# Dividing attention outputs by their row sums: the reciprocal moved from ScalarE to GpSimd

## The chip, the cores and the metric

The kernel runs on one core of a Trainium2 chip. The metric is the device time of one execution in microseconds (us). Shown are the median of three runs, their spread, and the span of one profiled execution.

## The reference, cut to what matters

A chain of six residual blocks works on x, 2 sequences of 1024 tokens with 128 features: mixture of experts, attention, the same mixture of experts again, a latent-attention block with its own routed experts, a scan block, and the latent-attention block again. The blocks that matter here are the three attentions with 16 heads and causal masks:

```python
attn = softmax(where(causal, q @ k.T * scale + bias, -inf), axis=-1)
out = attn @ v                 # per head
x = x + out.reshape(b, s, d) @ W_O
...
att = softmax(where(tril, q @ k.T / sqrt(64), -inf), axis=-1)
y = (att @ v).reshape(b, t, H * D) @ Wo
```

Each softmax ends in a division by the row's sum. The kernel does that division last, on the outputs of `attn @ v`.

## The kernel before, in words

The program is written engine by engine, and each engine has a fixed order of instructions with semaphores between engines. For the attention stages the order comes from a planner, the classes `Plan` (line 95 on), `First` (the first attention) and `Late` (the experts after it, the two latent attentions, their experts and the scan). `Plan.quad` (line 131) lists the tasks of four heads ("a quad", number n) of one batch, in two phases ph of 512 queries. `Plan.simulate` (line 224) then plays the engines forward with the costs in `COST` (lines 108 and 328), in us, and the priorities in `ORDER` (lines 113 and 342), and keeps the order that comes out. `Late.TABLE` (line 340) says which activation table a ScalarE task needs; `Late.extra` (line 588) charges 1.3 for a change.

There are 24 quads, 8 in `First` and 16 in `Late`, so 48 phases. In each phase:

- TensorE makes unmasked scores to find each query's maximum (`un`, line 1277), VectorE reduces them (`red`, lines 1396 to 1403), TensorE turns the maxima (`turn`, line 1343), VectorE copies them (`ct`, line 1418) and two small DMAs on SP's queue put them beside the queries (`crow`, line 1442).
- TensorE makes the scores with the maximum taken off (`sc`, line 1291, with masks in line 1298), in pairs of PSUM banks of which there are three, shared with `un`. ScalarE takes the exponential of each pair into PR (`exp`, line 1369), 18 per quad and 432 in all. TensorE multiplies PR with the values (`pv`, line 1337); a column of ones in the values gives the row sum in the same PSUM tile.
- ScalarE copies the result to OS (`ev`, line 1377); VectorE's shuffle spreads each head's row sum over its 32 partitions into RX (`den`, line 1422); ScalarE takes RX's logarithm (`ln`, line 1381) and the exponential of minus that (`rx`, line 1385); GpSimd multiplies OS with RX (`on`, line 1437), into ON for even quads and in place for odd ones.
- After each odd quad TensorE projects both quads with two matmuls (`proj`, lines 1348 and 1349), and VectorE adds the result to the residual (`add`, line 1430).

An `ev` of an odd quad waits for the `on` of the even one before it, in the same phase, since both use OS. An even quad's `on` waits for the projection before it. On GpSimd, `on` shares the queue with `vs` (copies of the values, line 1527) in `First`, and in `Late` with the gating of experts (`et`, line 2262), rotations of the queries (`rot`, lines 2282 to 2285), low parts of fp16 splits (`xql`, `xl`) and the scan's products. All elementwise tiles here are 128 partitions by 512 or 1024 elements.

```python
            last = ("pv", n, ph, NGRP[ph] - 1)
            self.take(("pv", n, ph, 0), "misc", add("ACT", "ev", ("ev", n, ph), last, ("on" if n % 2 else "proj", n - 1, ph) if n else None))
            add("DVE", "den", ("den", n, ph), ("ev", n, ph))
            add("ACT", "ln", ("ln", n, ph), ("den", n, ph))
            add("ACT", "rx", ("rx", n, ph), ("ln", n, ph))
            add("POOL", "on", ("on", n, ph), ("rx", n, ph), ("proj", n - 1, ph) if n and n % 2 == 0 else None)
```

Of the kernel before, what the change touches and what calls it, by code (L numbers as in the profile page):

```python
# [23 lines left out]
ALU = mybir.AluOpType  # L24
ACT = mybir.ActivationFunctionType
AX = mybir.AxisListType

P = 128
# [71 lines left out]
class Plan:  # L100
# [4 lines left out]
    LATENT = False  # L105
    ROOM = {"pair": 3, "misc": 2, "nr": 2}
    SINGLE = ("turn", "proj")
    COST = {"turn": 0.2, "proj": 1.9, "m4": 0.25, "ct": 0.27, "crow": 1.2, "den": 0.72, "ev": 0.58, "ln": 0.63,
            "rx": 0.63, "on": 1.27, "add": 0.68, "qk": 1.75, "qkh": 1.02, "qkl": 1.22, "val": 1.9, "vc": 1.02, "vs": 0.5,
            "put": 7.0}  # L110
    LAND = {"crow": 2.5, "put": 4.0}
    MODE = {"sc": 1, "un": 1, "pv": 2}
    ORDER = {"ACT": ("qkh", "ev", "vc", "ln", "exp", "rx"),
             "DVE": ("ct", "m4", "den", "qkl", "add", "red"),
             "POOL": ("vs", "on"),
             "SP": ("crow", "put")}
# [6 lines left out]
    def add(self, eng, stream, task, *needs):  # L123
        self.needs[task] = [x for x in needs if x is not None]
        self.streams.setdefault((eng, stream), []).append(task)
        return task
# [4 lines left out]
    def quad(self, n, units, values, first_add=(None, None)):  # L131

        add = self.add
        for ph in range(2):
            for i in range(len(UNITS[ph])):
                u = add("PE", "un", ("un", n, ph, i), *units)
                r = add("DVE", "red", ("red", n, ph, i), u)
                self.take(u, "pair", r)
            add("DVE", "m4", ("m4", n, ph), r, ("turn", n - 1, ph) if n else None)
            tn = add("PE", "turn", ("turn", n, ph), ("m4", n, ph))  # L140
            self.take(tn, "misc", add("DVE", "ct", ("ct", n, ph), tn, ("crow", n - 1, ph) if n else None))
            add("SP", "crow", ("crow", n, ph), ("ct", n, ph))
            for i in range(len(SCORES[ph])):
                g = group_of_step(ph, i)
                old = self.group_before(group(n, ph, g) - NPR)
                s = add("PE", "sc", ("sc", n, ph, i), ("crow", n, ph))
                x = add("ACT", "exp", ("exp", n, ph, i), s, ("pv",) + old if old else self.values_room(group(n, ph, g)))
                self.take(s, "pair", x)
                if i % 2 == 0 and i + 1 < len(SCORES[ph]):
                    continue  # L150
                need = [x]
                if g == 0:
                    need += values
                add("PE", "pv", ("pv", n, ph, g), *need)
            last = ("pv", n, ph, NGRP[ph] - 1)
            self.take(("pv", n, ph, 0), "misc", add("ACT", "ev", ("ev", n, ph), last, ("on" if n % 2 else "proj", n - 1, ph) if n else None))
            add("DVE", "den", ("den", n, ph), ("ev", n, ph))
            add("ACT", "ln", ("ln", n, ph), ("den", n, ph))
            add("ACT", "rx", ("rx", n, ph), ("ln", n, ph))
            add("POOL", "on", ("on", n, ph), ("rx", n, ph), ("proj", n - 1, ph) if n and n % 2 == 0 else None)  # L160
            if n % 2 == 0:
                continue
            s = add("PE", "proj", ("proj", n, ph), ("on", n, ph))
            self.take(s, "misc", add("DVE", "add", ("add", n, ph), s, first_add[ph]))
# [156 lines left out]
class Late(Plan):  # L321
# [17 lines left out]
    LAND = dict(Plan.LAND, egb=2.4, wl1=4.0, wl2=3.0, kput=3.0, st=2.5)  # L339
    TABLE = {"eg": "gelu", "si": "silu", "sg": "sigmoid", "th": "sigmoid", "ge": "gelu", "exp": "exp", "ln": "exp", "rx": "exp",  # L340
             "vln": "exp", "vex": "exp", "ve0": "exp", "rex": "exp", "de": "exp", "dl": "exp", "dx": "exp"}
    ORDER = {"ACT": ("exh", "ewh", "eg", "roth", "krh", "lath", "kh", "vc", "ev", "rex", "sq", "vln", "vex", "si", "xp", "sg", "th", "ab", "de",
                     "dl", "dx", "ge", "xh", "ln", "exp", "rx", "xqh", "wqh", "ve0", "gwh"),
             "DVE": ("exl", "ewl", "eup", "eh", "ct", "m4", "den", "cen", "scl", "scb", "rt", "gtc", "hf", "gt", "mya", "mup", "cv", "dt0", "dts", "bd",
                     "scn", "st2", "st3", "oup", "fya", "fup", "krot", "krl", "kl", "ksw", "km", "rotd", "rotl", "swp",
                     "bt", "latl", "cp", "add", "red", "gwl", "wql"),
# [287 lines left out]
def build_program(nc, a, out):  # L634
    with ExitStack() as ctx:
# [219 lines left out]
        def pool_const(pool):  # L855
# [33 lines left out]
            for e in range(E):  # L889
                ins = pool.memset(desc[:, e:e + 1], float(E - e))  # L890
            pool.memset(epsc[:, 0:1], EPS)
            ins = pool.memset(epsc[:, 1:2], EPS * EPS)
            ins.then_inc(s_const, 1)

# [296 lines left out]
        def hq(ph):  # L1191
            return slice(ph * TT, (ph + 1) * TT)
# [109 lines left out]
        def pe_attn(pe, lat, c, plan, task):  # L1302
# [37 lines left out]
            elif kind == "turn":  # L1340
                n, ph = args
                pe.wait_ge(sig["m4"], c("m4", n, ph))
                pe.transpose(single(plan, task)[0:16, 0:P], M4[:, ph, :], identf[:, :]).then_inc(sig["turn"], 1)
            else:
                n, ph = args
                pe.wait_ge(sig["on"], c("on", n, ph))
                w_o = wo1 if lat else wo0
                pe.matmul(single(plan, task), w_o[:, n % NQ - 1, :], ON[:, hq(ph)], start=True, stop=False)
                pe.matmul(single(plan, task), w_o[:, n % NQ, :], OS[:, hq(ph)], start=False, stop=True).then_inc(sig["proj"], 1)

        def act_attn(act, lat, c, plan, task):
            kind, args = task[0], task[1:]
            if kind == "exp":
# [13 lines left out]
                    dst = PR[:, slot % NPR, :, 0:256].rearrange("a (p w) t -> a w p t", w=2)  # L1367
                    src = ps[pair][:, :, :].rearrange("a w (p t) -> a w p t", p=2)
                act.activation(dst, src, ACT.Exp, scale=0.125 if lat else 1.0).then_inc(sig["exp"], 1)  # L1369
            elif kind == "ev":  # L1370
                n, ph = args
                act.wait_ge(sig["pv"], c("pv", n, ph, NGRP[ph] - 1))
                if n % 2:
                    act.wait_ge(sig["on"], c("on", n - 1, ph))
                elif n:
                    act.wait_ge(sig["proj"], c("proj", n - 1, ph))
                act.copy(OS[:, hq(ph)], single(plan, ("pv", n, ph, 0))).then_inc(sig["ev"], 1)
            elif kind == "ln":
                n, ph = args
                act.wait_ge(sig["den"], c("den", n, ph))  # L1380
                act.activation(RX[:, hq(ph)], RX[:, hq(ph)], ACT.Ln).then_inc(sig["ln"], 1)
            else:
                n, ph = args
                act.wait_ge(sig["ln"], c("ln", n, ph))
                act.activation(RX[:, hq(ph)], RX[:, hq(ph)], ACT.Exp, scale=-1.0).then_inc(sig["rx"], 1)  # L1385

        def dve_attn(dve, lat, c, plan, task):
            kind, args = task[0], task[1:]
# [42 lines left out]

        def pool_attn(pool, c, plan, task):
            n, ph = task[1:]
            pool.wait_ge(sig["rx"], c("rx", n, ph))
            if n and n % 2 == 0:
                pool.wait_ge(sig["proj"], c("proj", n - 1, ph))
            pool.tensor_tensor((ON, OS)[n % 2][:, hq(ph)], OS[:, hq(ph)], RX[:, hq(ph)], ALU.mult).then_inc(sig["on"], 1)  # L1437

        def sp_crow(sp, lat, c, n, ph):
# [1058 lines left out]
```

## Time and profile before

| what | value |
|---|---|
| median of 3 runs | 1519.11 us (1517.02 to 1519.50) |
| profiled execution | 1519.04 us |
| its span on the core | 1517.1 us |
| instructions | 27015 |
| mean granted TensorE clock | 0.953 of full |
| busy: TensorE, VectorE, ScalarE, GpSimd | 1358.6, 1001.6, 884.7, 403.6 us |

The span runs from the first to the last instruction in the profile; 1.9 us of the execution lie around it. Busy times of different engines overlap. "Idle before" counts the time in which an engine stood still ahead of a group of instructions, and the name behind the arrow is what ended it. PE is TensorE's matmul, PEld its weight load, DVE is VectorE, ACT ScalarE, POOL GpSimd; L1437 is line 1437 of the kernel.

### The profile page before, as it was taken

Reading aid. Unit: us, or ns where it says so; the run is one execution under the profiler, and the core shown is the slowest. Engines: PE = TensorE matmul, PEld = TensorE weight load, DVE = VectorE, ACT = ScalarE, POOL = GpSimd, SP = SyncE. Lnnn points to the kernel's source line nnn. Section 1 sums busy time; section 2 is a strip of 40 time slices with the busy share of each in tenths; the row PEclk is TensorE's granted clock in tenths of the full one; section 3 lists DMA queues with packets and bytes.
Section 4 is the critical chain, followed back from the end, with each engine's and each line's share of the span. In section 5 each row is a group of like instructions: output and inputs, shape, how many; then the busy total and the mean of one; then the engine's idle time right before and its main releaser. Section 6 shows DMA issues by size and latency. Waiting matters only on the chain.

```text
span 1517.1 us, 27015 instructions
## 1 busy us (share of the span) xinstructions
PE 1358.6 (90%) x10934; PEld 571.3 (38%) x10934; DVE 1001.6 (66%) x1517; ACT 884.7 (58%) x1112; POOL 403.6 (27%) x331
## 2 busy tenths in 40 slices
PE   4999977888887899998999998999889999999997
PEld 2544432333333344443333433334333343334342
DVE  4333348888862545677887677686887788586735
ACT  2322333677786365254656558886678865665572
POOL 5365500010101466552222203112213032112000
PEclk8799986999998899998999999999899999999999
DMA  5632001100000632110101101102001001101100
GB/s 163 113 56 56 1 16 38 38 2 2 2 2 0 136 84 59 29 30 12 36 11 21 22 1 22 23 1 54 0 1 22 15 19 22 29 1 30 22 1 14
DMA packets 30279, 45.80 MB, mean 30 GB/s; under 512 B 5886, under 2 KB 10686, under 8 KB 30110
## 3 DMA queue, kind: packets, MB, share of 16 engines
q1 hardware_dynamic: 30156, 44.08, 13.5%
q8 instruction: 87, 1.43, 0.4%
q14 instruction: 36, 0.29, 0.1%
HBM read 25.39 MB, written 1.18 MB: 18 GB/s over the span
## 4 chain that ended last, share of the span: by engine, by line
PE 73%; ACT 10%; DVE 9%; issue 6%; POOL 1%; SPq 1%; DMA 0%; POOLq 0%; ACTq 0%; DVEq 0%
PE ps L1291 14%; PE ps L1337 12%; ACT PR L1369 6%; PE ps L1277 5%; PE ps L1643 4%; PE ps L1079 3%; PE ps L1644 3%; PE ps L1645 3%; PE ps L1669 3%; DVE BM L1403 2%; PE ps L1757 2%; PE ps L1269 2%; PE ps L1093 2%; PE ps L1094 2%; PE ps L1095 2%
## 5 line engine op out<-in xcount | busy, mean ns | idle before, releaser
L1369 ACT ACTIVATE PR<-ps 128x1024 f32<-128x1024 f32 x432 | 433.6, 1024 | 247.5 <-PE ps L1298 144.6
L1403 DVE TENSOR_REDUCE BM<-ps 128x2 f32<-128x1024 f32 (+2 forms) x384 | 348.4, 949 | 54.5 <-PE ps L1277 53.5
L1291 PE MATMUL ps<-QS,KS 48*128 48x512 f16 (+7 forms) x2688 | 307.0, 330 | 44.4 <-ACT PR L1369 35.2
L1337 PE MATMUL ps<-PR,VS 128*32 128x512 f32 (+3 forms) x2304 | 237.7, 505 | 3.3 <-ACT PR L1369 2.8
L1277 PE MATMUL ps<-KS,QS 48*128 48x128 f16 (+2 forms) x1728 | 168.1, 282 | 29.8 <-DVE BM L1403 19.7
L1291 PEld LDWEIGHTS ps<-QS,KS 48*128 48x128 f16 (+1 forms) x2688 | 107.2, 95 | 218.5 <-ACT PR L1369 104.1
L1396 DVE TENSOR_REDUCE BM<-ps 128x8 f32<-128x1024 f32 x96 | 116.7, 1219 | 42.6 <-PE ps L1277 42.2
L1277 PEld LDWEIGHTS ps<-KS,QS 48*128 48x128 f16 x1728 | 69.9, 96 | 158.2 <-DVE BM L1403 69.1
L1071 POOL TENSOR_TENSOR HL<-HL,PR 128x512 f32<-128x512 f32 x64 | 82.7, 1293 | 84.1 <-ACT HL L1117 83.2
L1147 DVE SCALAR_TENSOR_TENSOR HL<-ps,HL 128x512 f32<-128x512 f32 x64 | 44.2, 691 | 87.0 <-POOL HL L1071 87.0
L2282 POOL TENSOR_TENSOR KS<-BT,HL 128x1024 f16<-128x1024 f32 x14 | 33.1, 2368 | 228.3 <-DMA QS<-KS 207.2
L1117 ACT ACTIVATE HL<-ps 128x512 f32<-128x512 f32 x64 | 38.2, 597 | 94.5 <-PE ps L1095 94.5
L1437 POOL TENSOR_TENSOR ON<-OS,RX 128x512 f32<-128x512 f32 x24 | 31.6, 1315 | 228.9 <-ACT RX L1385 228.9
L1298 PE MATMUL ps<-maskB,idA 64*128 64x64 bf16 (+1 forms) x1536 | 92.3, 203 | 0.0
L1815 ACT ACTIVATE HL<-ps 128x512 f32<-128x512 f32 x64 | 37.7, 597 | 84.3 <-PE ps L1645 84.2
L1298 PEld LDWEIGHTS ps<-maskB,idA 64*128 64x128 bf16 x1536 | 71.2, 95 | 33.6 <-issue 2.6
L1337 PEld LDWEIGHTS ps<-PR,VS 128*32 128x32 f32 x2304 | 52.3, 109 | 81.6 <-issue 61.5
L1437 POOL TENSOR_TENSOR OS<-OS,RX 128x512 f32<-128x512 f32 x24 | 32.0, 1333 | 159.2 <-ACT RX L1385 159.2
L1079 PE MATMUL ps<-HL,WM 128*128 128x512 f32 x128 | 65.1, 593 | 0.2 <-DVE HL L1147 0.2
L1399 DVE TENSOR_REDUCE BM<-ps 128x4 f32<-128x1024 f32 x48 | 58.3, 1215 | 7.5 <-PE ps L1277 7.4
L1269 PE MATMUL ps<-maskA,idA 64*128 64x256 bf16 (+1 forms) x384 | 49.6, 337 | 9.6 <-issue 5.9
L1800 ACT ACT_TABLE_LOAD x43 | 55.2, 1283 | 0.8
(306 smaller groups left out, 2193.5 us busy)
## 6 DMA issues: line engine op xcount, KB each, us to landing
PR<-gates SPq DMA_DIRECT2D x32, 512.0 KB, 13.9
QS<-KS SPq DMA_DIRECT2D x64, 128.0 KB
QS<-KS SPq DMA_DIRECT2D x64, 64.0 KB
WM<-W_in SPq DMA_DIRECT2D x1, 2048.0 KB, 9.3
QS<-HL SPq DMA_DIRECT2D x48, 32.0 KB
KS<-HL SPq DMA_DIRECT2D x48, 32.0 KB
QS<-CT SPq DMA_DIRECT2D x96, 2.0 KB
KS<-KS SPq DMA_DIRECT2D x8, 128.0 KB, 2.4
```

The costliest lines, as they stand in the source:

```text
L1071: pool.tensor_tensor(GE0[:, u % 3, :], GE0[:, u % 3, :], GB[:, t % 2, e, :], ALU.mult).then_inc(s_gg, 1)
L1079: pe.matmul(bank(t % 2), w_out[:, i // 2, i % 2, :], HF[:, v % NHF, :], start=(i == 0), stop=(i == PER - 1)).then_inc(s_out, 1)
L1269: pe.matmul(ps[pair][:, w, :].rearrange("p (i c) -> p i c", c=P)[:, :, at_:P], idA[rows, half, :], maskA[rows, half, at_:P].unsqueeze(1).t ...
L1277: ins = pe.matmul(ps[pair][:, w, off:off + nk * P], QS[rows, sl, qt * P:(qt + 1) * P], KS[rows, ks, k0 * P:(k0 + nk) * P], start=not diag, ...
L1291: ins = pe.matmul(ps[pair][:, w, off:off + cols], KS[rows, ks, kt * P:(kt + 1) * P], QS[rows, qs, (ph + 1) * TT - cols:(ph + 1) * TT], sta ...
L1298: ins = pe.matmul(ps[pair][:, w, off:off + wide], idA[rows, half, :], maskB[rows, half, 0:wide], start=False, stop=(half == 1))
L1337: ins = pe.matmul(dst[32 * j:32 * j + 32, TT - cols:TT], v, PR[:, buf, j, off:off + cols], start=(g == 0), stop=(g == NGRP[ph] - 1))
L1369: act.activation(dst, src, ACT.Exp, scale=0.125 if lat else 1.0).then_inc(sig["exp"], 1)
L1396: ins = dve.tensor_reduce(BM[:, ph, p, :, :, 0], bnk[:, :, :].rearrange("a w (i c) -> a w i c", c=P), AX.X, ALU.max)
L1403: ins = dve.tensor_reduce(BM[:, ph, p, :, qt - 4 * ph, part], bnk[:, :, off:off + nk * P], AX.X, ALU.max)
L1437: pool.tensor_tensor((ON, OS)[n % 2][:, hq(ph)], OS[:, hq(ph)], RX[:, hq(ph)], ALU.mult).then_inc(sig["on"], 1)
L1643: pe.matmul(dst, w[0], x[0], start=True, stop=False)
```

## The change

The tasks `ln` and `rx` leave ScalarE's queue and the planner. `on` becomes two instructions on GpSimd: RX to the power of -1 in place, with a column of -1.0 spread over the tile as second operand, and then the product as before, which waits for the power by the same semaphore. That semaphore now counts two for each `on`, so the waits on it are doubled. In the planner `on` costs 2.3 instead of 1.27 and needs `den` directly. One fill writes the -1.0 at the start.

```diff
--- before.py
+++ after.py
@@ -105,12 +105,11 @@
     LATENT = False
     ROOM = {"pair": 3, "misc": 2, "nr": 2}
     SINGLE = ("turn", "proj")
-    COST = {"turn": 0.2, "proj": 1.9, "m4": 0.25, "ct": 0.27, "crow": 1.2, "den": 0.72, "ev": 0.58, "ln": 0.63,
-            "rx": 0.63, "on": 1.27, "add": 0.68, "qk": 1.75, "qkh": 1.02, "qkl": 1.22, "val": 1.9, "vc": 1.02, "vs": 0.5,
+    COST = {"turn": 0.2, "proj": 1.9, "m4": 0.25, "ct": 0.27, "crow": 1.2, "den": 0.72, "ev": 0.58, "on": 2.3, "add": 0.68, "qk": 1.75, "qkh": 1.02, "qkl": 1.22, "val": 1.9, "vc": 1.02, "vs": 0.5,
             "put": 7.0}
     LAND = {"crow": 2.5, "put": 4.0}
     MODE = {"sc": 1, "un": 1, "pv": 2}
-    ORDER = {"ACT": ("qkh", "ev", "vc", "ln", "exp", "rx"),
+    ORDER = {"ACT": ("qkh", "ev", "vc", "exp"),
              "DVE": ("ct", "m4", "den", "qkl", "add", "red"),
              "POOL": ("vs", "on"),
              "SP": ("crow", "put")}
@@ -155,9 +154,7 @@
             last = ("pv", n, ph, NGRP[ph] - 1)
             self.take(("pv", n, ph, 0), "misc", add("ACT", "ev", ("ev", n, ph), last, ("on" if n % 2 else "proj", n - 1, ph) if n else None))
             add("DVE", "den", ("den", n, ph), ("ev", n, ph))
-            add("ACT", "ln", ("ln", n, ph), ("den", n, ph))
-            add("ACT", "rx", ("rx", n, ph), ("ln", n, ph))
-            add("POOL", "on", ("on", n, ph), ("rx", n, ph), ("proj", n - 1, ph) if n and n % 2 == 0 else None)
+            add("POOL", "on", ("on", n, ph), ("den", n, ph), ("proj", n - 1, ph) if n and n % 2 == 0 else None)
             if n % 2 == 0:
                 continue
             s = add("PE", "proj", ("proj", n, ph), ("on", n, ph))
@@ -337,10 +334,10 @@
         "scn": 2.3, "st2": 1.3, "st3": 1.3, "outp": 0.87, "oup": 0.75, "f1": 0.87, "ge": 0.68, "f2": 1.75, "fya": 0.75,
         "fup": 0.7, "tr": 0.5, "egb": 2.7, "wl1": 4.5, "wl2": 1.2, "exh": 0.6, "exl": 0.69, "ewh": 0.68, "ewl": 0.69, "eu": 1.28, "eg": 0.68, "eh": 0.75, "et": 1.3, "ed": 0.87, "eup": 0.75, "cp": 0.69, "st": 0.6})
     LAND = dict(Plan.LAND, egb=2.4, wl1=4.0, wl2=3.0, kput=3.0, st=2.5)
-    TABLE = {"eg": "gelu", "si": "silu", "sg": "sigmoid", "th": "sigmoid", "ge": "gelu", "exp": "exp", "ln": "exp", "rx": "exp",
+    TABLE = {"eg": "gelu", "si": "silu", "sg": "sigmoid", "th": "sigmoid", "ge": "gelu", "exp": "exp",
              "vln": "exp", "vex": "exp", "ve0": "exp", "rex": "exp", "de": "exp", "dl": "exp", "dx": "exp"}
     ORDER = {"ACT": ("exh", "ewh", "eg", "roth", "krh", "lath", "kh", "vc", "ev", "rex", "sq", "vln", "vex", "si", "xp", "sg", "th", "ab", "de",
-                     "dl", "dx", "ge", "xh", "ln", "exp", "rx", "xqh", "wqh", "ve0", "gwh"),
+                     "dl", "dx", "ge", "xh", "exp", "xqh", "wqh", "ve0", "gwh"),
              "DVE": ("exl", "ewl", "eup", "eh", "ct", "m4", "den", "cen", "scl", "scb", "rt", "gtc", "hf", "gt", "mya", "mup", "cv", "dt0", "dts", "bd",
                      "scn", "st2", "st3", "oup", "fya", "fup", "krot", "krl", "kl", "ksw", "km", "rotd", "rotl", "swp",
                      "bt", "latl", "cp", "add", "red", "gwl", "wql"),
@@ -889,6 +886,7 @@
             for e in range(E):
                 ins = pool.memset(desc[:, e:e + 1], float(E - e))
             pool.memset(epsc[:, 0:1], EPS)
+            pool.memset(epsc[:, 3:4], -1.0)
             ins = pool.memset(epsc[:, 1:2], EPS * EPS)
             ins.then_inc(s_const, 1)
 
@@ -1343,7 +1341,7 @@
                 pe.transpose(single(plan, task)[0:16, 0:P], M4[:, ph, :], identf[:, :]).then_inc(sig["turn"], 1)
             else:
                 n, ph = args
-                pe.wait_ge(sig["on"], c("on", n, ph))
+                pe.wait_ge(sig["on"], 2 * c("on", n, ph))
                 w_o = wo1 if lat else wo0
                 pe.matmul(single(plan, task), w_o[:, n % NQ - 1, :], ON[:, hq(ph)], start=True, stop=False)
                 pe.matmul(single(plan, task), w_o[:, n % NQ, :], OS[:, hq(ph)], start=False, stop=True).then_inc(sig["proj"], 1)
@@ -1367,22 +1365,14 @@
                     dst = PR[:, slot % NPR, :, 0:256].rearrange("a (p w) t -> a w p t", w=2)
                     src = ps[pair][:, :, :].rearrange("a w (p t) -> a w p t", p=2)
                 act.activation(dst, src, ACT.Exp, scale=0.125 if lat else 1.0).then_inc(sig["exp"], 1)
-            elif kind == "ev":
+            else:
                 n, ph = args
                 act.wait_ge(sig["pv"], c("pv", n, ph, NGRP[ph] - 1))
                 if n % 2:
-                    act.wait_ge(sig["on"], c("on", n - 1, ph))
+                    act.wait_ge(sig["on"], 2 * c("on", n - 1, ph))
                 elif n:
                     act.wait_ge(sig["proj"], c("proj", n - 1, ph))
                 act.copy(OS[:, hq(ph)], single(plan, ("pv", n, ph, 0))).then_inc(sig["ev"], 1)
-            elif kind == "ln":
-                n, ph = args
-                act.wait_ge(sig["den"], c("den", n, ph))
-                act.activation(RX[:, hq(ph)], RX[:, hq(ph)], ACT.Ln).then_inc(sig["ln"], 1)
-            else:
-                n, ph = args
-                act.wait_ge(sig["ln"], c("ln", n, ph))
-                act.activation(RX[:, hq(ph)], RX[:, hq(ph)], ACT.Exp, scale=-1.0).then_inc(sig["rx"], 1)
 
         def dve_attn(dve, lat, c, plan, task):
             kind, args = task[0], task[1:]
@@ -1431,9 +1421,11 @@
 
         def pool_attn(pool, c, plan, task):
             n, ph = task[1:]
-            pool.wait_ge(sig["rx"], c("rx", n, ph))
+            pool.wait_ge(sig["den"], c("den", n, ph))
             if n and n % 2 == 0:
                 pool.wait_ge(sig["proj"], c("proj", n - 1, ph))
+            pool.tensor_tensor(RX[:, hq(ph)], RX[:, hq(ph)], epsc[:, 3:4].to_broadcast([P, TT]), ALU.pow).then_inc(sig["on"], 1)
+            pool.wait_ge(sig["on"], 2 * c("on", n, ph) - 1)
             pool.tensor_tensor((ON, OS)[n % 2][:, hq(ph)], OS[:, hq(ph)], RX[:, hq(ph)], ALU.mult).then_inc(sig["on"], 1)
 
         def sp_crow(sp, lat, c, n, ph):
```

## Rows read from the trace of the kernel before

**Rows 1.** The page: busy time by engine, and the chain that ended last by engine

```profile
PE 1358.6 (90%) x10934; PEld 571.3 (38%) x10934; DVE 1001.6 (66%) x1517; ACT 884.7 (58%) x1112; POOL 403.6 (27%) x331
...
PE 73%; ACT 10%; DVE 9%; issue 6%; POOL 1%; SPq 1%; DMA 0%; POOLq 0%; ACTq 0%; DVEq 0%
```

**Rows 2.** Waits, whole span: who waited for whom, us in total, times, longest

```profile
PEld ps L1291 <- ACT PR L1369: 104.1, 142, 2.7
...
PE ps L1291 <- ACT PR L1369: 35.2, 51, 2.4
...
PE ps L1348 <- POOL OS L1437: 4.8, 3, 2.5
```

**Rows 3.** Groups by line, shapes apart: count | busy us, mean ns | idle before

```profile
L1369 ACT ACTIVATE PR<-ps 128x1024 f32<-128x1024 f32 x432 | 433.6, 1024 | 247.5 <-PE ps L1298 144.6 <-PE ps L1291 100.8
...
L1422 DVE STREAM_SHUFFLE RX<-OS 128x512 f32<-128x512 f32 x48 | 35.0, 730 | 0.1
...
L1437 POOL TENSOR_TENSOR OS<-OS,RX 128x512 f32<-128x512 f32 x24 | 32.0, 1333 | 159.2 <-ACT RX L1385 159.2
L1437 POOL TENSOR_TENSOR ON<-OS,RX 128x512 f32<-128x512 f32 x24 | 31.6, 1315 | 228.9 <-ACT RX L1385 228.9
...
L1381 ACT ACTIVATE RX<-RX 128x512 f32<-128x512 f32 x48 | 30.1, 628 | 7.5 <-DVE RX L1422 7.5
L1385 ACT ACTIVATE RX<-RX 128x512 f32<-128x512 f32 x48 | 30.0, 626 | 0.7
```

**Rows 4.** Timeline, first and last odd quad's phase: start us, us, engine, line, operation

```profile
287.19 0.71 DVE L1422 STREAM_SHUFFLE RX<-OS 128x512 f32<-128x512 f32 x1
...
288.69 0.62 ACT L1381 ACTIVATE RX<-RX 128x512 f32<-128x512 f32 x1
...
290.23 0.62 ACT L1385 ACTIVATE RX<-RX 128x512 f32<-128x512 f32 x1
...
290.93 1.28 POOL L1437 TENSOR_TENSOR OS<-OS,RX 128x512 f32<-128x512 f32 x1 [6.94 <-ACT RX L1385]
...
292.46 0.30 PEld L1348 LDWEIGHTS ps<-ON,wo 128*128 128x128 f32 x2 [0.43 <-issue]
...
1483.18 1.27 POOL L1437 TENSOR_TENSOR OS<-OS,RX 128x512 f32<-128x512 f32 x1 [12.87 <-ACT RX L1385]
...
1487.06 0.19 PEld L1348 LDWEIGHTS ps<-ON,wo 128*128 128x128 f32 x1 [0.24 <-issue]
```

**Rows 5.** The chain of waits in order of time: start us, us, what

```profile
288.69 0.62 ACT RX L1381
...
465.43 1.26 POOL ON L1437
...
934.99 1.28 ACT L1800
936.28 0.63 ACT RX L1381
...
1459.49 1.29 POOL OS L1437
...
1481.81 0.64 ACT RX L1381
1482.47 0.64 ACT RX L1385
```

**Rows 6.** Groups by line on GpSimd: a fill, and an operation behind its own engine's

```profile
L2285 POOL TENSOR_TENSOR KS<-BT,KS 128x1024 f16<-128x1024 f32 x14 | 29.9, 2137 | 1.1
...
L1510 POOL MEMSET KS<- 128x512 f32 x16 | 7.4, 515 | 0.0
```

**Rows 7.** One line, L1437: duration ns min/median/max, first and last start us

```profile
L1437 POOL TENSOR_TENSOR OS<-OS,RX x24: 1262/1272/2720, 290.9 to 1483.2; 128x512 f32<-128x512 f32 x24
```

**Rows 8.** Timeline: the slowest product, and VectorE beside it

```profile
1184.89 2.72 POOL L1437 TENSOR_TENSOR OS<-OS,RX 128x512 f32<-128x512 f32 x1 [8.99 <-ACT RX L1385]
1184.96 0.73 DVE L2044 SCALAR_TENSOR_TENSOR XN<-XN,colp,VS 128x512 f32<-128x512 f32 x1
```

## The prediction

> **What bounds the kernel now.** I read the page's busy table first and the chain of waits second. TensorE is busy for 90% of the span and ScalarE for 58%, and the chain that ended last runs for 73% on TensorE and for 10% on ScalarE [rows 1]. So ScalarE as a whole has room, and what leaves it is worth only what it delays. That shows in the waits: TensorE's weight loads and matmuls of the scores wait 104.1 and 35.2 us in all for the exponentials of line 1369, because a score buffer comes free only when ScalarE has read it [rows 2]. The groups by line give the pieces that the change touches: the logarithm takes 628 ns and the exponential of minus it 626 ns, 48 times each; the shuffle that feeds them 730 ns; the product on GpSimd 1315 and 1333 ns on the mean in its two forms [rows 3]. GpSimd sits idle for 228.9 and 159.2 us in front of these products, waiting for ScalarE's result, so it has time to give.
>
> One instance in order of time shows the latency [rows 4]. The shuffle ends at 287.90; the logarithm starts at 288.69, behind an exponential of the scores; its partner only at 290.23, behind the next one; the product starts at 290.93, 3.03 us after the shuffle's end. Over the 46 instances in which shuffle and product pair off plainly this latency is 1.4 to 11.6 us, with a median of 2.85. The projection's weight load follows at 292.46, 0.25 us after the product's end (292.21); in the last instance it starts at 1487.06, 2.61 us after 1484.45. The 24 phases of odd quads have such a projection behind them; in 15 of them it follows within 1.9 us, in 9 it has 2.3 us or more to spare. Its place in TensorE's queue is fixed by the plan.
>
> **The change part by part.** *Removed:* 48 logarithms and 48 exponentials, 48 x (0.628 + 0.626) = 60.2 us of ScalarE's work, 6.8% of its 884.7 us. The chain, read piece by piece, holds twelve pieces of them, the first at 288.69 and the last at 1482.47, 4.9 us together; eight of them are 0.52 to 0.64 us long, four under 0.1 [rows 5]. That is the direct gain. The indirect one is that exponentials of the scores stand 0.63 or 1.25 us earlier when nothing is pushed between them. If TensorE's 139.3 us of waiting for them [rows 2] fell in proportion to ScalarE's work, that would be 0.068 x 139.3 = 9.5 us; if those slots only turn into idle time of ScalarE, it is nothing.
>
> *Added:* 48 powers on GpSimd, 128x512 in fp32, each with the product waiting for its semaphore. The trace has no power on any engine, so its price is bounded by neighbours. The same engine's fill of 128x512 takes 515 ns, which computes nothing and reads nothing: the lower end [rows 6]. The product of the same shape and with two inputs takes a median of 1272 ns [rows 7]: the nearest row, if a power is one pass over the data like a product. The upper end is a power made of many arithmetic passes' worth of work, a logarithm and an exponential in one; ten products are 12.7 us. I take 1.27 us. In favour: the plan's costs for the old pieces (ln 0.63, den 0.72, on 1.27) lie on the trace's 0.628, 0.730 and 1.272, and its new "on" of 2.3, read the same way, leaves 1.03 us for the power. A figure in a plan is weak evidence, and both ends stay in the range. The handover from one GpSimd operation to the next that waits for it costs about 1.1 / 14 = 0.08 us, from line 2285 [rows 6]; a handover from another engine is 0.08 too, from 290.85 to 290.93 [rows 4].
>
> At 1.27 us the product starts about 1.27 + 0.08 + 0.08 = 1.4 us after the shuffle's end, the same as the fastest instances now and 1.45 us before the median one. GpSimd's work grows by 61 us on 403.6. What is queued behind it there: the copies of values in the first attention, and rotations and low parts (lines 2282, 2275) in the second; the 387 us in which GpSimd stands idle ahead of the products alone cover that [rows 3]. If the cover went in a phase, the operation behind would be late by one power, 1.3 us, and with it the DMAs or matmuls that it feeds; no DMA is added or moved, on no queue. Where the product itself is on the path, the power is now in front of it. That is so at three places, 465.43, 1459.49 and 1483.18 [rows 4, 5]; 3 x 1.27 = 3.8 us at worst, against the 1.25 us each that goes there and is in the 4.9 already. One more fill at the start is a single column, against 512 in the fill of 515 ns, and counts as nothing.
>
> *Moved:* the planner loses two tasks per phase and so writes new fixed orders for all engines; the table loads of ScalarE that stand right in front of a logarithm, as the 1.28 us at 934.99 [rows 5], may move or go. Nothing in the trace prices a new order. I take zero with 6 us to either side, about the size of two exchanges of an exponential per stage.
>
> The sum: 4.9 direct, between 0 and 9.5 indirect, minus 0 to 3.8 gives a gain of 1.1 to 14.4 us. I take 7: nearer the middle than either end, since the chain shows the pieces on the path in every stage. The profiled execution took 1519.04 us, its span 1517.1 and 1.9 around it, and the median shown is 1519.11, so either base gives 1512.
>
> **A rule against it.** The product row shows a simple two-input pass at 1272 ns. The Trainium skill, GPSIMD Engine Reference, section 3.1, says that bodies of up to two operations per element are bound by the port, and from three on by instruction slots at about three operations a cycle, so a function of dozens of operations costs a multiple of a product. By this the power is several us and the kernel gets slower; no run here shows it yet, and it is the first rival.
>
> A second row points at a side effect: one product took 2.72 us at 1184.89, twice the median, while VectorE worked on a two-operand instruction at 1184.96 [rows 8]. The Trainium skill, SBUF — State Buffer, "SBUF: two separate sides", says that the two engines take a shared port pair exclusively, for a whole instruction; by that rule a long power would also hold up VectorE's two-operand instructions. The trace agrees as far as one doubled product goes.
>
> **The rivals.** *1. The power is long (chance 0.38), slower.* The price decides from about 2.8 us, the present median latency, because beyond it the product ends later than now while its projection's place in TensorE's queue is fixed. TensorE stalls at the projection by the power's excess over that instance's latency and slack. Taken over the 24 projections one by one, each with its own latency and slack as in [rows 4], a power of 6.4 us (five products) makes 45 us of stall, one of 12.7 us 160 us. The ends of stages, with up to three powers in a row, add some 5 to 20 us, and about 5 us come back from ScalarE: 1519 + 45 + 8 - 5 = 1567 for five products, near 1690 for ten. For it: every GpSimd row here is a copy, a fill or one simple operation per element, and ScalarE needs two passes for the same function. Against it: the plan's 2.3 us.
>
> *2. The freed time was hidden anyway (chance 0.11), no change.* ScalarE's idle time is 42% of the span, and TensorE, 73% of the chain, keeps its work. Then only part of the 4.9 us comes back, a power at the stage ends takes it again: 1518. Against it are the pieces on the chain.
>
> *3. The new order is worse (chance 0.06), slower.* The planner may put scores behind a longer neighbour in some phases; 8 us lost against 4 gained: 1523. For it speaks that TensorE is 90% busy, so an order has little room to be worse in; against it, that the plan has fewer tasks to place.
>
> **How the numbers follow.** The forecast, a short power with a gain, has 0.45: 1512, with 1503 to 1516 as its own range (gain of 14.4 and the order's share below, 3 us above). About 0.2%, 3 us, is what a measurement here can tell from no change. Faster is the forecast plus a little luck of the order in the others: 0.46. Same is rival 2 and the small ends of the rest: 0.13. Slower is rival 1 and 3 less what falls within 3 us: 0.41. The range reaches from 1500 up to 1590, which takes in a power of up to some seven products and leaves out the rest of rival 1, about 0.16, and 0.02 below.
>
> **What would show it.** The power's own row at line 1437's neighbour: about 1.3 us means forecast, over 3 us rival 1. In the first case the product starts 1.4 us after each shuffle, ScalarE's busy time is 825 us, and TensorE's waits for exponentials are below 139 us. In the second there are waits of TensorE at line 1348 for GpSimd, far above the present 4.8 us in three waits [rows 2], and idle time of the score matmuls beside them. Rival 2 would show the same waits for exponentials under less ScalarE work; rival 3 other waits, for VectorE's reductions. A power over 2.8 us would make the forecast wrong by itself.

## The result and the profile after

The changed kernel takes 5032.8 us (median of 4 runs, 5030.9 to 5034.9) against 1518.7 us for the kernel before: a ratio of 3.314, 95% interval 3.309 to 3.320. The profiled execution has a span of 5032.5 us.

The page of the changed kernel, busy times and chain, against [rows 1]:

```profile
PE 1436.2 (29%) x10934; PEld 594.8 (12%) x10934; DVE 1002.3 (20%) x1517; ACT 824.4 (16%) x1008; POOL 4330.3 (86%) x380
...
POOL 81%; PE 14%; DVE 3%; ACT 1%; issue 1%; SPq 0%; DMA 0%; POOLq 0%; DVEq 0%; ACTq 0%
POOL RX L1427 78%; PE ps L1289 1%; PE ps L1335 1%; PE ps L1077 1%; PE ps L1661 1%; PE ps L1346 1%; DVE BM L1393 1%; PE ps L1635 1%; PE ps L1347 1%; PE ps L1636 1%; PE ps L1637 1%; POOL OS L1429 1%; PE ps L1275 1%; PE ps L1091 1%; PE ps L1092 1%
```

GpSimd went from 404 to 4330 us of work, and one line, the power, holds 78% of the chain. ScalarE's busy time fell by 60.3 us, the sum that was worked out, but in part for another reason, as the section on the prediction shows. The same kernel, by line (durations as minimum, median and maximum in ns):

```profile
L1412 DVE STREAM_SHUFFLE RX<-OS x48: 708/723/749, 244.7 to 4916.0; 128x512 f32<-128x512 f32 x48
L1427 POOL TENSOR_TENSOR RX<-RX,epsc x48: 81915/81916/82370, 245.5 to 4916.8; 128x512 f32<-128x512 f32 x48
L1429 POOL TENSOR_TENSOR ON<-OS,RX x24: 1260/1262/1262, 327.5 to 4807.8; 128x512 f32<-128x512 f32 x24
L1429 POOL TENSOR_TENSOR OS<-OS,RX x24: 1260/1262/1262, 494.3 to 4998.8; 128x512 f32<-128x512 f32 x24
```

One power takes 81.9 us, all 48 of them within 0.5 us of each other. The product of the same shape behind it takes 1.26 us. Where that goes is in the waits of the changed kernel (us in total, times, longest), against [rows 2]:

```profile
PE ps L1346 <- POOL OS L1429: 2857.4, 24, 165.2
ACT PR L1367 <- PE ps L1289: 1945.3, 136, 170.6
...
ACT OS L1375 <- POOL ON L1429: 427.6, 9, 61.9
...
POOL RX L1427 <- DVE RX L1412: 292.9, 22, 34.6
```

TensorE stood at each of the 24 projections for GpSimd, 119 us on the mean, and everything behind the projection in its fixed order stood too. Two powers in a row explain the longest, 165 us. GpSimd itself waited for a shuffle only 293 us in all: it is now the bound. One piece of its timeline shows the series:

```profile
329.07 81.92 POOL L1427 TENSOR_TENSOR RX<-RX,epsc 128x512 f32<-128x512 f32 x1
411.07 1.26 POOL L1429 TENSOR_TENSOR ON<-OS,RX 128x512 f32<-128x512 f32 x1
412.29 81.92 POOL L1427 TENSOR_TENSOR RX<-RX,epsc 128x512 f32<-128x512 f32 x1
494.28 1.26 POOL L1429 TENSOR_TENSOR OS<-OS,RX 128x512 f32<-128x512 f32 x1
```

The sum closes: 48 x 81.93 = 3932.5 us of powers, 78% of 5032.5, lie on the chain practically in full. The span grew by 3515.4 us, so some 417 us of the old span now run underneath powers. TensorE's clock is lower as well in the stretches in which it waits, and its 10934 matmuls take 1436.2 us against 1358.6 [rows 1]. The stretches (in us; busy time of PE, PEld, DVE, ACT and POOL with counts, then granted clock, DMA share and GB/s):

```profile
245.00:1700.00 1455.00, 229.96 (x2278) 86.01 (x2278) 175.35 (x232) 153.20 (x168) 1333.31 (x40) 0.57 0.01 2
1700.00:1897.00 197.00, 183.89 (x810) 80.00 (x811) 116.20 (x171) 90.26 (x141) 104.49 (x76) 0.95 0.31 65
1897.00:5032.00 3135.00, 815.02 (x6966) 326.78 (x6962) 607.43 (x963) 505.14 (x582) 2788.15 (x135) 0.63 0.02 5
```

In both stretches with powers the mean granted clock is 0.57 and 0.63, between the two levels of 1.2 and 2.4 GHz; between them no power runs (one ends before 1700 and the next starts at 1898.0), and it is 0.95.

### The profile page after: what moved, and what is told of

Same layout as the page of the kernel before. It is cut to its first block, busy times and chain, and to the rows that moved or that the text cites. A ratio compares the mean times of both kernels' runs of the same rounds, so it can differ in the third digit from the quotient of the medians.

```text
span 5032.5 us, 26961 instructions
## 1 busy us (share of the span) xinstructions
PE 1436.2 (29%) x10934; PEld 594.8 (12%) x10934; DVE 1002.3 (20%) x1517; ACT 824.4 (16%) x1008; POOL 4330.3 (86%) x380
## 4 chain that ended last, share of the span: by engine, by line
POOL 81%; PE 14%; DVE 3%; ACT 1%; issue 1%; SPq 0%; DMA 0%; POOLq 0%; DVEq 0%; ACTq 0%
POOL RX L1427 78%; PE ps L1289 1%; PE ps L1335 1%; PE ps L1077 1%; PE ps L1661 1%; PE ps L1346 1%; DVE BM L1393 1%; PE ps L1635 1%; PE ps L1347 1%; PE ps L1636 1%; PE ps L1637 1%; POOL OS L1429 1%; PE ps L1275 1%; PE ps L1091 1%; PE ps L1092 1%
## 5 line engine op out<-in xcount | busy, mean ns | idle before, releaser
L1427 POOL TENSOR_TENSOR RX<-RX,epsc 128x512 f32<-128x512 f32 x48 | 3932.5, 81928 | 293.0 <-DVE RX L1412 292.9
L1346 PE MATMUL ps<-ON,wo 128*128 128x512 f32 x48 | 49.1, 1127 | 2857.4 <-POOL OS L1429 2857.4
L1289 PE MATMUL ps<-QS,KS 48*128 48x512 f16 (+7 forms) x2688 | 322.4, 343 | 487.8 <-ACT PR L1367 360.2
L1420 DVE TENSOR_TENSOR YA<-YA,ps 128x512 f32<-128x512 f32 x16 | 11.0, 688 | 1935.8 <-PE ps L1347 1935.8
L1346 PEld LDWEIGHTS ps<-ON,wo 128*128 128x128 f32 x48 | 12.0, 310 | 2873.7 <-issue 2873.7
L1335 PE MATMUL ps<-PR,VS 128*32 128x512 f32 (+3 forms) x2304 | 248.8, 523 | 52.9 <-ACT PR L1367 52.6
L1821 ACT ACTIVATE VS<-YA 128x512 f32<-128x512 f32 x20 | 12.5, 627 | 900.1 <-DVE YA L1420 811.2
L1069 POOL TENSOR_TENSOR HL<-HL,PR 128x512 f32<-128x512 f32 x64 | 83.0, 1297 | 85.7 <-ACT HL L1115 82.7
L1375 ACT COPY OS<-ps 128x512 f32<-128x512 f32 x48 | 28.1, 585 | 447.4 <-POOL ON L1429 427.6
L2090 DVE SCALAR_TENSOR_TENSOR BT<-ps,WM 128x1024 f32<-128x1024 f32 x32 | 38.1, 1215 | 182.5 <-POOL KS L2277 164.0
L2254 POOL TENSOR_TENSOR HL<-HL,PR 128x512 f32<-128x512 f32 x30 | 40.7, 1371 | 36.7 <-DVE HL L2015 30.2
```

What stands on the lines that cost most here:

```text
L1069: pool.tensor_tensor(GE0[:, u % 3, :], GE0[:, u % 3, :], GB[:, t % 2, e, :], ALU.mult).then_inc(s_gg, 1)
L1289: ins = pe.matmul(ps[pair][:, w, off:off + cols], KS[rows, ks, kt * P:(kt + 1) * P], QS[rows, qs, (ph + 1) * TT - cols:(ph + 1) * TT], sta ...
L1335: ins = pe.matmul(dst[32 * j:32 * j + 32, TT - cols:TT], v, PR[:, buf, j, off:off + cols], start=(g == 0), stop=(g == NGRP[ph] - 1))
L1427: pool.tensor_tensor(RX[:, hq(ph)], RX[:, hq(ph)], epsc[:, 3:4].to_broadcast([P, TT]), ALU.pow).then_inc(sig["on"], 1)
```

## The experiments

The theory after the result: the power's duration on GpSimd is the whole loss. The rivals: the new order of all engines, which the plan writes when two tasks per phase go, costs by itself; and ScalarE's freed time was never worth anything.

**A cheap pass in the power's place.** The same instruction, with a product for the power:

```diff
-            pool.tensor_tensor(RX[:, hq(ph)], RX[:, hq(ph)], epsc[:, 3:4].to_broadcast([P, TT]), ALU.pow)
+            pool.tensor_tensor(RX[:, hq(ph)], RX[:, hq(ph)], epsc[:, 3:4].to_broadcast([P, TT]), ALU.mult)
```

> The changed kernel with the power replaced by a product with the same operands (outputs are then not divided by the row sums). Theory A: the whole loss is the power's own 81.9 us on GpSimd; with a pass of 1.27 us in its place the other terms of my sum hold, and the kernel takes 1505 to 1516 us, faster than before. Rival B: the freed 60 us of ScalarE were hidden and the pass on GpSimd takes back what little they give: 1516 to 1522. Rival C: the new order or the handover on GpSimd costs by itself: over 1522.

Measured: 1531.4 us against 1516.1, ratio 1.0095 (1.0065 to 1.0126). Rival C. The operation alone accounts for 5032.8 down to 1531.4, but what is left is still slower than before. Its line in that kernel:

```profile
L1427 POOL TENSOR_TENSOR RX<-RX,epsc x48: 1038/1039/1909, 245.6 to 1495.6; 128x512 f32<-128x512 f32 x48
```

A product with the column spread over the tile takes 1.04 us, and 1.04 + 1.27 = 2.3, the plan's figure for the pair. The figure fits a product, not a power.

**The old order without ScalarE's two passes.** In the kernel before, the `ln` and `rx` tasks issue nothing:

```diff
-                act.wait_ge(sig["den"], c("den", n, ph))
-                act.activation(RX[:, hq(ph)], RX[:, hq(ph)], ACT.Ln).then_inc(sig["ln"], 1)
+                pass
...
-                act.wait_ge(sig["ln"], c("ln", n, ph))
-                act.activation(RX[:, hq(ph)], RX[:, hq(ph)], ACT.Exp, scale=-1.0).then_inc(sig["rx"], 1)
+                pass
...
-            pool.wait_ge(sig["rx"], c("rx", n, ph))
+            pool.wait_ge(sig["den"], c("den", n, ph))
```

> The kernel before, with its own order, but ScalarE issues nothing for the logarithm and the exponential and the product waits for the shuffle (outputs are multiplied by the row sums, not divided). Theory A: the freed ScalarE time is worth 4.9 us and up to 9.5 more: 1505 to 1514. Rival B, all of it was hidden: 1517 to 1520. Beside the run with a product for the power it tells the new order and the extra pass apart from the freed time: equal times mean that both cost nothing.

Measured: 1505.4 us, ratio 0.9924 (0.9899 to 0.9950). The freed time has a value, 11.5 us by the ratio, with no replacement for the division at all. In this order a way of taking the two passes off ScalarE can hardly bring more.

**The new order alone, the old order with the pass, and another plan.** Three kernels separate the two changes that e1 holds. The first drops the power and its wait from the changed kernel (the semaphore then counts one for each `on` again); the second adds the cheap pass and its wait to the old order; the third is the first with the plan's cost of `on` at 1.27.

```diff
             pool.wait_ge(sig["den"], c("den", n, ph))
...
-            pool.tensor_tensor(RX[:, hq(ph)], RX[:, hq(ph)], epsc[:, 3:4].to_broadcast([P, TT]), ALU.pow).then_inc(sig["on"], 1)
-            pool.wait_ge(sig["on"], 2 * c("on", n, ph) - 1)
```

> The changed kernel's new order with no power and nothing in its place: the product waits for the shuffle (outputs are multiplied by the row sums). The run with a product for the power took 1531 and the old order without ScalarE's two passes 1505. If the new order itself is what costs those 26 us, this takes 1525 to 1532; if the extra GpSimd pass of 1.04 us does, it takes 1503 to 1509.

Measured: ratio 1.0072 (1.0045 to 1.0099), 1526.3 us against 1518.4.

> The old order, nothing on ScalarE for the two passes, and on GpSimd the product with -1.0 ahead of the product with the outputs (outputs not divided). If the order is what costs, 1504 to 1511, since a pass of 1.04 us is less than the 2.85 us it replaces; if the extra pass does, 1525 to 1532.

Measured: ratio 0.9998 (0.9980 to 1.0015), 1516.3 us. This lies between the two expectations: the pass costs something too.

```diff
-            "on": 2.3,
+            "on": 1.27,
```

> As the new order alone, with nothing for the power, but planned with 1.27 us for the product instead of 2.3. If a shorter planned cost undoes the loss, 1500 to 1510; if any order that the planner writes without the two ScalarE tasks is as bad, 1525 to 1535; anything between says that an order alone moves the time by about 1%, either way.

Measured: ratio 1.0135 (1.0110 to 1.0160), 1536.8 us, 1.8 us above the second expectation: the shorter planned cost does not undo the loss.

All four kernels without a power and without ScalarE's two passes, as ratios to the kernel before:

| order | nothing added | cheap pass on GpSimd |
|---|---|---|
| old | 0.9924 | 0.9998 |
| new, planned with 2.3 | 1.0072 | 1.0095 |
| new, planned with 1.27 | 1.0135 | not run |

The new order costs 1.5% (22 us) in the first column. The pass costs 0.7% in the old order (by the intervals 0.4 to 1.1) and 0.2% in the new one, which the intervals do not tell from nothing. Where the new order loses shows in TensorE's waits for the exponentials of the scores. In the old order without the two passes they are

```profile
PEld ps L1291 <- ACT PR L1369: 97.5, 137, 1.8
PE ps L1291 <- ACT PR L1369: 33.1, 49, 1.5
```

and in the new one

```profile
PEld ps L1289 <- ACT PR L1367: 124.6, 151, 1.6
PE ps L1289 <- ACT PR L1367: 50.7, 71, 1.1
```

That is 175.3 us against 130.6, and 139.3 in the kernel before [rows 2]. With less for ScalarE to do, TensorE waits longer for it, because the scores stand at other places. Waits for VectorE's reductions fall in turn, so that the 45 us are not the loss itself; the places were not followed one by one.

What the pass's 0.7% in the old order is made of is less clear. The chain of waits, between the first attention and the second mixture of experts, in the old order without the pass:

```profile
470.11 3.70 PE ps L920 x8
473.81 3.45 PE ps L923 x8
...
479.27 4.27 PE ps L961 x32
```

and with it:

```profile
471.36 5.98 PE ps L921 x8
477.34 3.45 PE ps L924 x8
...
482.80 7.01 PE ps L962 x32
```

The same 8 and 32 matmuls take 2.3 and 2.7 us longer, with only 1.25 us between the starts. The granted clock over 465 to 500 is 0.76 in the old order without the pass, and 1.00 over the 8 matmuls of line 920 (columns as above):

```profile
465.00:500.00 35.00, 21.43 (x74) 10.43 (x73) 18.01 (x40) 12.19 (x22) 2.54 (x4) 0.76 0.11 22
469.00:476.00 7.00, 6.02 (x15) 2.77 (x15) 3.50 (x6) 3.32 (x6) 0.00 (x0) 1.00 0.00 0
```

With it, it is 0.66, and at the lower level, 0.50, under most of the same 8:

```profile
465.00:500.00 35.00, 20.78 (x57) 11.74 (x55) 15.41 (x37) 10.57 (x19) 3.57 (x5) 0.66 0.00 1
469.20:476.00 6.80, 5.83 (x8) 2.06 (x7) 2.12 (x4) 0.73 (x2) 0.00 (x0) 0.50 0.00 0
```

So 5.0 of the 14.1 us between these two executions (1522.6 and 1508.4 us) are matmuls at the lower clock. The medians differ by 11.0 only, and the execution with the pass is the slowest of its kernel's twelve. Whether the lower clock comes with the pass or with that one execution isn't shown, and the rest was not followed.

**A power on fewer columns.** The power on 40 of the 512 columns, the others left undivided:

```diff
-            pool.tensor_tensor(RX[:, hq(ph)], RX[:, hq(ph)], epsc[:, 3:4].to_broadcast([P, TT]), ALU.pow)
+            pool.tensor_tensor(RX[:, ph * TT:ph * TT + 40], RX[:, ph * TT:ph * TT + 40], epsc[:, 3:4].to_broadcast([P, 40]), ALU.pow)
```

> The changed kernel with the power on 40 of the 512 columns (the others stay undivided). If the price is 160 ns a column (81.9 us over 512) with little fixed cost, a power takes 6.4 us; theory A, by the working of the prediction's first rival (45 us of stall, 8 at stage ends, 5 back): 1560 to 1575. A rival: the price is mostly fixed per instruction, then a power stays above 40 us and the kernel above 2900.

Measured: 1682.2 us, ratio 1.109 (1.104 to 1.114), and the line:

```profile
L1427 POOL TENSOR_TENSOR RX<-RX,epsc x48: 6740/6743/7726, 244.3 to 1645.2; 128x40 f32<-128x40 f32 x48
```

The price is (81916 - 6743) / 472 = 159.3 ns a column and 0.37 us fixed. The duration came as expected; the total did not, it is 107 us above the expected band. Two runs went after that: the same power in the old order, from which the prediction had read its latencies, and the same power with the plan told the true length (`"on": 8.1`).

> The old order with the power on 40 columns (6.74 us). The prediction's rival read latency and slack from this very order and gave 1567 for 6.4 us. If its working was right and the miss in the run with 40 columns (1682) was the new order's tighter place for the projection, 1560 to 1580; if reading 24 instances one by one leaves out what the stalls push behind them, over 1620.

Measured: 1641.8 us, ratio 1.081 (1.079 to 1.084). Over 1620, so the working itself was short. TensorE's waits of that kernel at the projection:

```profile
PE ps L1349 <- POOL OS L1438: 99.5, 20, 12.0
```

Worked as in the prediction, but with 6.75 us, the stalls should have summed to 51. The timeline of the first projection shows what was left out:

```profile
280.20 6.75 POOL L1436 TENSOR_TENSOR RX<-RX,epsc 128x40 f32<-128x40 f32 x1 [1.56 <-DVE RX L1421]
287.03 1.28 POOL L1438 TENSOR_TENSOR ON<-OS,RX 128x512 f32<-128x512 f32 x1
287.07 0.71 DVE L1421 STREAM_SHUFFLE RX<-OS 128x512 f32<-128x512 f32 x1
288.27 6.75 POOL L1436 TENSOR_TENSOR RX<-RX,epsc 128x40 f32<-128x40 f32 x1
295.09 1.26 POOL L1438 TENSOR_TENSOR OS<-OS,RX 128x512 f32<-128x512 f32 x1
296.47 0.50 PEld L1349 LDWEIGHTS ps<-ON,wo 128*128 128x128 f32 x2 [4.55 <-issue]
```

In the first attention phases come in pairs, an even quad's second and an odd quad's first, about 8 us apart. A power and a product are 8.1 us, so the second power starts only when the first pair is done, 0.5 us after its own shuffle's end here. Later the queue is longer. In the last latent attention a power stands behind the three instructions of a rotation, and the next power behind that one:

```profile
1473.42 0.74 DVE L1421 STREAM_SHUFFLE RX<-OS 128x512 f32<-128x512 f32 x1
1476.85 2.12 POOL L2286 TENSOR_TENSOR KS<-BT,KS 128x1024 f16<-128x1024 f32 x1
1478.93 6.75 POOL L1436 TENSOR_TENSOR RX<-RX,epsc 128x40 f32<-128x40 f32 x1
1486.98 6.74 POOL L1436 TENSOR_TENSOR RX<-RX,epsc 128x40 f32<-128x40 f32 x1
1495.18 0.50 PEld L1349 LDWEIGHTS ps<-ON,wo 128*128 128x128 f32 x2 [12.48 <-issue]
```

The shuffle ends at 1474.16 and its power starts 12.8 us later. In all, 22 of the 48 powers stand behind other work of GpSimd, 108 us together, 56 of them behind the product of the phase before and 44 behind rotations; with the pass of 1.04 us in the same order it is 13 of 48 and 55 us. The stalls came to 99.5 us in place of 51, so 48 of the 69 us that were missing (1642 against the 1573 that the prediction's working gives) are at the projection. The other 21 were not followed.

> The power on 40 columns again (6.74 us measured, 1682 us with the plan's cost of 2.3), now with the plan told 8.1 us for power and product. If the stall comes from TensorE's projection standing in a place planned for 2.3 us, the order now leaves room and the kernel takes 1525 to 1560; if a latency of 8 us can't be hidden in any order, it stays above 1640.

Measured: 1565.5 us, ratio 1.030 (1.027 to 1.034), just above the expected band. TensorE waits at the projection in three places for 12.8 us in all, against 21 places and 121.3 us in the run planned with 2.3. The waits of the replanned kernel:

```profile
PE ps L1346 <- POOL OS L1429: 12.8, 3, 9.7
```

and of the one planned with 2.3:

```profile
PE ps L1346 <- POOL OS L1429: 121.3, 21, 9.7
```

So of the 11% that 6.7 us cost, 8 points go with the order that is planned for them, more than the 0.6 points by which the orders planned with 2.3 and with 1.27 differ. An 8 us latency can mostly be hidden here, if the plan knows of it.

**The full power in the old order.**

> The old order with the full power of 512 columns ahead of each product, everything else as before the change (outputs divided as in the changed kernel). If the power's 81.9 us on GpSimd are all that makes 5033, and the new order's share is the 20 us seen without it, this takes 4950 to 5050. If the new order made it worse by placing the projections tightly, this is under 4900.

Measured: 5011.2 us, ratio 3.303 (3.296 to 3.309), 21.6 us below the changed kernel, about as much as the two orders differ without a power (22 us). The chain holds 78% of power here too. At this length the order makes 0.4% of the time; the power makes the rest.

**What the power's time depends on.** Two more kernels, one execution each: the power on 8 partitions instead of 128, and an exponent of +1.0.

```diff
-            pool.memset(epsc[:, 3:4], -1.0)
+            pool.memset(epsc[:, 3:4], 1.0)
```

> The changed kernel with the power on 8 of the 128 partitions, all 512 columns. If the engine works through the 128 partitions of a column together, a power still takes about 82 us; if it does them one after the other in each of its cores, 8 partitions take about half of what 16 do, some 41 us; and if in sixteen groups over all partitions, about 5 us.

> The changed kernel with the exponent +1.0 in place of -1.0 (outputs are multiplied by the row sums). If the time of a power depends on its exponent, or the engine has a short way for simple ones, its 81.9 us change; if not they stay within 1 us, and with them 5033.

Measured: 5032.9 and 5032.0 us, and the line of the power on 8 partitions:

```profile
L1427 POOL TENSOR_TENSOR RX<-RX,epsc x48: 81906/81907/82371, 244.4 to 4915.1; 8x512 f32<-8x512 f32 x48
```

and with the exponent of +1.0:

```profile
L1427 POOL TENSOR_TENSOR RX<-RX,epsc x48: 81917/81917/82383, 243.2 to 4914.5; 128x512 f32<-128x512 f32 x48
```

Neither matters. The time follows the columns, and neither of these two exponents has a shorter way than the other.

**Another engine for the reciprocal.** VectorE takes it right behind the shuffle, planned at 2.0 us for both (and the product at 1.27), and nothing is added on GpSimd:

```diff
+                dve.wait_ge(sig["den"], 2 * c("den", n, ph) - 1)
+                dve.reciprocal(RX[:, hq(ph)], RX[:, hq(ph)]).then_inc(sig["den"], 1)
```

> The changed kernel with the power taken out and VectorE taking the reciprocal of the shuffled sums right behind the shuffle (planned at 2.0 us for both); the product stays on GpSimd. A reciprocal of 0.7 us, as VectorE's other passes of 128x512, would give 1508 to 1520, since VectorE is 66% busy; one of some 3 us adds 144 us to VectorE and should cost 20 to 80 us: 1540 to 1600.

Measured: 1647.4 us, ratio 1.086 (1.083 to 1.089). The reciprocal's line:

```profile
L1414 DVE RECIPROCAL RX<-RX x48: 3352/3353/3355, 248.6 to 1604.6; 128x512 f32<-128x512 f32 x48
```

3.35 us, over four times the shuffle of that size, and 161 us more work for VectorE, whose reductions feed the scores. The rise is 131 us, above both expectations; the line holds 7% of that kernel's chain, and TensorE waits 27.3 us at the projection. Shuffle and reciprocal take 4.1 us where the plan has 2.0, so a part of the 131 us may be the order's, as with the power on 40 columns; a plan with the true length was not run. The two passes on ScalarE at 1.25 us are the cheapest reciprocal that ran here.

## Why the prediction was wrong, point by point

**The power's price** is the step that failed. The prediction took 1.27 us, "if a power is one pass over the data like a product", and the power is 81.9, 65 times that. The upper end of 12.7 us was too low as well, by a factor of 6.5, so the range could not hold the time. Both ends came from counting passes of products; nothing in the trace bounded an operation that the engine had never been seen to do, and the range should have said so. The support, the plan's 2.3, was read as a measured figure. By the run with a product in its place it equals the cost of two products (1.04 + 1.27). A number in a planner says what its writer expected.

The forecast's direction rested on that step. The rival with a long power named the mechanism that happened: the product late, TensorE standing at the projection at line 1348 (1346 now). Its sign was right and its size wrong twice over: by the price, and by adding the stalls one at a time. At 6.75 us in the old order it would have given about 1573 with its own working (51 instead of 45 of stall); 1642 was measured. At 81.9 us the same working gives 1774 us of stall, and the old order with the full power waited 2720.5 us at the projection. Powers queue on GpSimd behind each other and behind rotations, which instances read one by one can't show. The prediction held that GpSimd's 387 us of idle time cover what is queued there; as a sum they would cover short powers, but the 22 waits above are for single places in the queue.

**The rule against it.** The Trainium skill, GPSIMD Engine Reference, section 3.1, says that from three operations per element on a body runs at roughly three operations a cycle. Read as the prediction reads it, that a function of many operations costs a multiple of a product, it pointed the right way. The trace agrees in kind, 81.9 us against 1.26. At the page's three operations a cycle and the 1.2 GHz that the page gives, 159.3 ns a column would be an estimated 570 operations; no run here shows that number.

**The shared port pair.** If a power kept VectorE's two-input instructions out for its whole length, they would stand for up to 82 us. The changed kernel shows otherwise; its chain has a power from 2572.48:

```profile
2572.48 81.92 POOL RX L1427
```

and VectorE's timeline has a combination of two SBUF tiles inside it:

```profile
2582.37 0.68 DVE L2169 SCALAR_TENSOR_TENSOR XT<-YA,XT 128x512 f32<-128x512 f32 x1
```

0.68 us is its ordinary time: of the line's eight instructions six run wholly inside powers, at 0.68 to 0.69 us, and two outside, at 0.69. VectorE's total is 1002.3 us against 1001.6. The Trainium skill, SBUF — State Buffer, "SBUF: two separate sides", gives the pair for the whole instruction to the one that starts first; for a power that does not hold, and the measurement decides. The doubled product that the prediction took as support doesn't fit either: it started first, at 1184.89, and VectorE's instruction began 0.07 us later and took its ordinary 0.73 us [rows 8]. What doubled the product isn't known.

**ScalarE's freed time**: 60.2 us of work were forecast and 60.3 came, which is luck. In the old order without the 96 passes ScalarE's busy time falls by 50.9 us only, from 884.7 to 833.8, since neighbouring records overlap a little ("busy" counts overlapping time once). The new order has 8 table loads fewer besides, 82 against 90, which are 10.3 us by themselves. The freed time's worth was put at 4.9 us direct and 0 to 9.5 more; 11.5 us were measured in the old order (7.6 to 15.3 by the interval), inside the bounds of 4.9 to 14.4 but for the interval's upper end. The indirect term's mechanism is there, since TensorE's waits for exponentials fell from 139.3 to 130.6 us. How much of the 11.5 is luck of the clock was not measured. The prediction also counted 1.25 us on the chain ahead of each of three products; the chain has 0.52, 0.53 and 1.28 there, and a fourth product at 466.70. That is a misreading of 1.4 us and changes nothing.

**The handover** on GpSimd: 0.08 us, right; the product's line shows 1.9 us of idle time before 24 of them.

**The new order** was taken as zero, 6 us to either side. It costs 22 us against the old order, nearly four times that bound and more than the freed time brings. That term alone would have turned the forecast: with a power as cheap as a product the change is 0.95% slower, not 0.5% faster. The forecast's own sign, waits for exponentials below 139 us, fails there too: they are 175.3 us in the new order without a power, with ScalarE's work down by 60. Rival 3 (1523) was the one to weigh more; it had 0.06, and looked for the waits at VectorE's reductions.

**No change by hidden time** (rival 2) is out: the old order without the passes is faster by 0.76%.

## What to carry to other kernels

An operation that the trace doesn't show has no price until it has run once at its size; neighbours bound copies and products, not functions, and a figure in a planner is an intention. Work moved to an idle engine is only free while each piece is shorter than the slack behind it, and pieces of neighbouring tiles queue, behind each other and behind the engine's other work. Where a planner writes the order, run the change's order without its operations first: here the new order cost 22 us where the freed engine time brought 11.5, and telling the planner a latency's true length took back most of what it cost.

## What was not expected of the hardware

- A power on GpSimd takes 81.9 us for 512 columns, on 128 or on 8 partitions, with exponents -1 and +1; with the 6.74 us for 40 columns that is 159.3 ns a column and 0.37 us fixed. Each head's sum fills 32 partitions of RX, so the 2048 different sums of a phase would fit 128 partitions by 16 columns, by that rate an estimated 2.9 us; the moves there and back were not tried.
- A product with a spread column as second operand takes 1.04 us, one with two full tiles 1.26 to 1.27.
- A GpSimd power of 82 us did not hold up VectorE's instructions with two SBUF inputs (0.68 us inside it).
- VectorE's reciprocal of 128x512 takes 3.35 us against 0.72 for a shuffle of the same tile.
- In two executions whose starts differ by 1.25 us at this place, the same 40 matmuls behind the first attention took 7.97 and 12.99 us, at granted clocks of 0.76 and 0.66 around them. What decides it was not shown. Differences under 0.5% (5.0 us are 0.3% here) need the granted clock looked at before they get a cause.
